# Attention passes: the last value products and the second copy-out moved into the next pass's first step

## What is computed

```python
q = q * cos + rotate_half(q) * sin
k = k * cos + rotate_half(k) * sin
scale = 1.0 / jnp.sqrt(jnp.asarray(HD, x.dtype))
attn = jnp.einsum('bhqd,bhkd->bhqk', q, k) * scale
attn = jax.nn.softmax(attn, axis=-1)
out = jnp.einsum('bhqk,bhkd->bhqd', attn, v)
```

## Time and profile before

| | |
|---|---|
| median of three runs | 950.13 us (949.09 to 950.76) |
| the profiled execution | 949.47 us |
| its span, first to last instruction | 947.7 us |
| PE busy | 794.8 us, 84% of the span |
| DVE busy | 788.2 us, 83% |
| ACT busy | 680.6 us, 72% |
| POOL busy | 238.7 us, 25% |
| mean granted TensorE clock | 0.933 of full speed |
| attention passes in the span | from 70 us (first exponential) to 430 us (last copy-out) |

### The profile page before, as it was taken

One profiled execution on the slowest core, in us unless ns is written; L12 is line 12 of the kernel. 1 busy time (PEld: TensorE's weight loads), 2 busy tenths in 40 slices (PEclk: granted clock), 3 DMA queues, 4 the chain that ended last, 5 costly groups with the idle time before them and its releaser, 6 DMA issues.

```text
span 947.7 us, 12535 instructions
## 1 busy us (share of the span) xinstructions
PE 794.8 (84%) x4272; PEld 419.4 (44%) x4272; DVE 788.2 (83%) x746; ACT 680.6 (72%) x1300; POOL 238.7 (25%) x133
## 2 busy tenths in 40 slices
PE   5689999999999999985575774766667876999998
PEld 3312222212222222223543553655666765888886
DVE  5998898878888988885868989999989764787864
ACT  2407777767777777784455796999996756888884
POOL 3800000000000000010100357897977411222200
PEclk9859999989999999998688788999998998999999
DMA  4313223230123110002101144455544202211111
GB/s 130 100 31 98 77 75 101 67 103 17 43 71 101 35 37 12 13 12 61 45 0 32 63 163 151 159 200 177 180 170 143 91 0 98 82 67 67 44 45 45
DMA packets 41688, 75.97 MB, mean 80 GB/s; under 512 B 7584, under 2 KB 25352, under 8 KB 40856
## 3 DMA queue, kind: packets, MB, share of 16 engines
q1 hardware_dynamic: 41624, 75.17, 24.8%
HBM read 64.99 MB, written 8.85 MB: 78 GB/s over the span
## 4 chain that ended last, share of the span: by engine, by line
PE 58%; DVE 17%; ACT 16%; issue 6%; DMA 2%; POOL 1%; ACTq 0%; DVEq 0%; POOLq 0%; SPq 0%
PE ps L1570 14%; PE ps L1591 13%; ACT dtb L1008 8%; PE ps L1541 7%; PE ps L1843 6%; PE ps L1844 6%; PE ps L1845 6%; ACT abar L982 4%; DVE nmax L1175 2%; DVE hst L1310 2%; ACT prob L884 1%; PE ps L1644 1%; PE ps L1743 1%; PE ps L1530 1%; PE ps L1718 1%
## 5 line engine op out<-in xcount | busy, mean ns | idle before, releaser
L884 ACT ACTIVATE prob<-ps 128x512 f32<-128x512 f32 x512 | 264.4, 607 | 98.8 <-PE ps L1570 96.3
L1178 DVE TENSOR_REDUCE nmax_k<-ps 128x2 f32<-128x1024 f32 x224 | 262.4, 1220 | 37.9 <-PE ps L1541 36.7
L1570 PE MATMUL ps<-qs,ks 96*128 96x512 bf16 x512 | 163.2, 391 | 5.6 <-ACT prob L884 4.1
L811 POOL TENSOR_TENSOR hc<-hst,cbr 128x1024 f32<-128x1024 f32 x63 | 153.0, 2452 | 42.4 <-DVE hst L1310 23.8
L1310 DVE TENSOR_TENSOR_SCAN hst<-abar,ps 128x1024 f32<-128x1024 f32 x64 | 143.1, 2274 | 6.6 <-PE ps L1743 4.2
L1591 PE MATMUL ps<-prob,vq 128*16 128x512 f32 x1024 | 134.2, 601 | 0.8 <-ACT prob L884 0.7
L1420 DVE TENSOR_TENSOR act_l<-act_t,act_h 128x1024 fp32r<-128x1024 f32 x64 | 86.4, 1362 | 39.1 <-ACT act_h L1106 39.1
L1570 PEld LDWEIGHTS ps<-qs,ks 96*128 96x128 bf16 x512 | 40.2, 97 | 164.6 <-ACT prob L884 109.7
L1008 ACT ACTIVATE dtb<-dtxt,bt 128x128 f32<-128x128 f32 x352 | 107.5, 398 | 0.9 <-PE ps L1743 0.9
L1743 PE MATMUL ps<-ident,dtb 128*128 128x128 f32 x352 | 56.3, 303 | 57.2 <-DVE hst L1310 43.0
L1102 ACT ACTIVATE act_t<-ps,b1t 128x512 f32<-128x512 f32 x128 | 81.8, 681 | 31.3 <-PE ps L1845 31.3
(11 more groups left out here) (204 smaller groups left out, 1118.5 us busy)
## 6 DMA issues: line engine op xcount, KB each, us to landing
cbr<-s_dram SPq DMA_DIRECT2D x64, 512.0 KB, 4.0
gate<-c_dram SPq DMA_DIRECT2D x6, 1024.0 KB, 4.7
qs<-q_dram SPq DMA_DIRECT2D x16, 288.0 KB
ks<-k_dram SPq DMA_DIRECT2D x48, 96.0 KB
o_dram<-o_sb SPq DMA_DIRECT2D x16, 256.0 KB, 2.1
wf<-in_L_ffn_w SPq DMA_DIRECT2D x8, 256.0 KB, 5.1
wfq<-in_L_ffn_w SPq DMA_DIRECT2D x8, 256.0 KB, 5.3
gate<-c_dram SPq DMA_DIRECT2D x4, 512.0 KB, 4.3
```

Source lines behind the costliest of these rows:

```text
L811: nc.gpsimd.tensor_tensor(hc[:, m % RING], hst[:, m % RING], cbr[:, m % RING], ALU.mult).then_inc(s_hc, 1)
L884: nc.scalar.activation(prob[:, n % 8], ps[:, 4 + (first + n) % 3], ACT.Exp, scale=ATT_SCALE).then_inc(s_exp, 1)
L1178: nc.vector.tensor_reduce(nmax_k[:, half, kk, 2 * pair:2 * pair + 2, qt], ps[:, 2 * pair:2 * pair + 2, :], AX.X, ALU.max, negate=True).the ...
L1570: nc.tensor.matmul(ps[:, 4 + (first + n) % 3], ks[p][:, kt // 4, j, kt % 4 * P:(kt % 4 + 1) * P], qs[p][:, half, j, :], start=True, stop=T ...
```

## The change

Three things are moved. On PE the products of step 15 are issued in step 0 of the next pass, after its fourth score product and second look-ahead tile, as those of every other step; the last pass alone keeps them at its end. The score products 0 to 2 of a later pass get the wait for the exponential three before. On ACT the copy of the second half is made after the four exponentials of the next pass's step 0, and steps 0 and 1 of a later pass wait for products as all others do. And ACT's loop is laid otherwise: pass 0 stands in front of it, its two rounds hold the passes 1 to 3 and 4 to 6, and pass 7 stands behind it. The number of passes in the loop's body (three) and of rounds (two) is as before. The bank of a score tile is the same as before for each.

```diff
-            def one_pass(it, first, between={}):
+            def one_pass(it, first, earlier, between={}):
...
-                        if j == 0 and s >= 2:
+                        if j == 0 and (s >= 2 or earlier):

                             act.wait_ge(s_pv, STEPS * it + s - 1)
...
+                    if s == 0 and earlier:
+                        evacuate(it - 1, 1)
                     if s == KT:
                         evacuate(it, 0)
-                evacuate(it, 1)
...
+            one_pass(0, 0, False)
             with act.Fori(0, PASSES // SETS) as r:
                 for p in range(SETS):
-                    one_pass(SETS * r + p, 4 * STEPS * p)
-            one_pass(PASSES - 2, 0)
+                    one_pass(SETS * r + p + 1, 4 * STEPS * (p + 1), True)
...
-            one_pass(PASSES - 1, 4 * STEPS, {
+            one_pass(PASSES - 1, 4 * STEPS * (PASSES - 1), True, {
                 8: lambda: norm_act(1, 0),
                 13: turned_weights})
+            evacuate(PASSES - 1, 1)
...
-                        if n >= 3:
+                        if n >= 3 or it:
                             pe.wait_ge(s_exp, 4 * STEPS * it + n - 2)
...
-                        if s >= 1 and j == (QUAD - 1 if todo else QUAD - 2):
-                            products(it, p, s - 1)
-                products(it, p, STEPS - 1)
+                        if j == (QUAD - 1 if todo else QUAD - 2):
+                            if s:
+                                products(it, p, s - 1)
+                            elif it:
+                                products(it - 1, (p - 1) % SETS, STEPS - 1)
+                if not more:
+                    products(it, p, STEPS - 1)
```

## The result

The changed kernel takes 945.71 us in the median of 8 runs (945.22 to 948.06), the kernel before 950.87 us in 8 (949.09 to 955.58). The ratio is 0.9951, with a 95% interval of 0.9935 to 0.9966: by the ratio 4.7 us faster, by the two medians 5.2, where 3.6 were forecast. In the profiled executions the span went from 947.7 to 944.1 us, by 3.6.

What follows compares the result with a forecast made beforehand. PE was taken to set the attention's pace, losing most at ACT's loop jump. Against the median, 950.13 - 3.59 (3.31 jump, 0.28 ordinary boundaries) = 946.5 us; range 944.9 to 949.2 us, own case 945.5 to 947.7.

Steps and rivals of the forecast that it cites:

- What bounds the kernel, and where the gain lies: PE sets attention's pace; the boundary from pass 2 to 3, at ACT's loop jump, costs 4.79 us more.
- The price of the jump in its new place: ACT's loop jump, now between passes 3 and 4, costs 1.48 us instead of 4.79: 3.31 us gained.
- The clock in the new gap: PE's gap of about 1.4 us at the moved jump leaves the clock at 1.00, no fall.
- Rival A: The clock falls in the new gap too: 2.54 us come back, gain 1.05, 949.1 us; chance 0.12.
- Ordinary boundaries: Seven pass boundaries go from 0.32 to 0.28 us each: 0.28 us gained; bounds 0 and 2.2.
- Passes in the loop and outside: Pass 6 gains up to 0.96 us inside ACT's loop, pass 0 loses as much outside: zero, within 0.3.
- The sum: Whole kernel: 949.47 - 3.31 - 0.28 = 945.9 us against the profiled execution, 946.5 against the median.
- All that comes behind shifts along: Everything behind the attention follows from its end and moves with it; no size of its own.
- D, late rows of maxima: A pass's first score, 0.98 us earlier, waits for its maxima: at full size 953.4 us, slower; chance 0.04.
- B, a second fetch: Jump dearer in its new place by a second or slower fetch: at most 2.1 us more, 948.6 us; chance 0.06.
- C, a hidden fetch: Fetch at the moved jump costs nothing: 4.79 + 0.28 us gained, 945.1 us; chance 0.08.
- E: Nothing moves: the jump's stall stays whole wherever it is and takes the clock down, 949.9 us; chance 0.03.

Runs made afterwards that it cites:

- b_one_round: Kernel before with ACT's loop over passes 0 to 5 made one round of six passes, no jump back; ratio to before 1.0008.
- b_relaid: Kernel before with only the changed kernel's loop layout (pass 0 in front, rounds of passes 1 to 3 and 4 to 6); ratio to before 0.9996.
- after_again: The changed kernel as it is, measured once more; ratio to before 0.9953.
- a_gap4_more: Changed kernel without ACT's loop and second wait, plus four copies and a shorter one before pass 4's first exponential; one run, attention 328.7 us.
- the pair without loop: Changed kernel and kernel before, each with ACT's passes written out and one wait per exponential; ratios to before 0.9918 and 0.9970.
- a_copy_only: Changed kernel with PE's old order, step 15's products at the pass's end, so only ACT's half of the change; ratio to before 1.0006.
- a_one_round: Changed kernel with ACT's loop made one round of six passes, no jump back; ratio to before 0.9987.
- a_one_wait: Changed kernel with ACT's passes 0 to 6 written out and no wait for products before a step's first exponential; 942.87 us, ratio to before 0.9918.
- a_gap5: a_one_wait with five added copies on ACT before pass 4's first exponential; one run, attention 334.7 us.
- a_gap5_again: Same program as a_gap5, run once more; one run, attention 329.0 us.
- b_products_only: Kernel before with only PE's half, step 15's products behind the third score of the next pass's step 0; one run, attention 350.0 us.

## Why the prediction was right, point by point

**What bounds the kernel, and where the gain lies.** Right. The distance between the copies of passes 2 and 3 went from 48.63 to 43.79 us, the 4.79 that the prediction had found and the 0.05 of an ordinary boundary, and b_one_round and b_relaid show that the jump is its cause: without a jump no such boundary, and with the jump elsewhere the price is elsewhere. One thing stays unshown: 2.5 of the 4.79 us were the fallen clock, and that is seen in one profiled execution of the kernel before. The fall does not come behind every such gap, so how much of it is in each of the other runs is not known.

**The price of the jump in its new place**: forecast 1.48, measured 1.0 (44.79 against 43.79), and 1.16 in after_again. ACT is idle for 1.70 us, where 2.1 were forecast, and PE for 0.89, where 1.4 were. The step that was off counted the fetch from the start of the instruction in front of the jump to the exponential behind, 2.72 us. Now it is shorter: the last of the four exponentials before starts at about 244.16 + 1.47 = 245.63, the next at 247.93, 2.30 us later (2.47 in after_again). The first instruction packet comes 1.7 us ahead of the exponential behind the jump at both places (204.3 before 206.05, and 246.2 before 247.93), but 1.0 us behind the start of the copy and 0.6 behind that of the last exponential: so if these packets are ACT's, the fetch begins earlier against ACT's work and is not shorter. An explanation is that the exponential in front waits in ACT's queue, so that the sequencer is at the jump before it starts, while the copy stood right before it; that was not tried by itself. This term alone is 0.48 us of gain above the forecast.

**The clock in the new gap.** No fall, as forecast, but the reason given was weak, and luck had a part. It argued from the scan's gaps of 1.48 and 1.80 us that one of 1.4 would do no harm. The gap came out at 0.89 (1.06 in after_again), shorter than any behind which a fall was seen; at the forecast's length one execution (a_gap4_more, 1.35) kept the clock, which by that run's expectation would make the step right, but behind 1.21 it fell three times in six. Rival A was worth more than 0.12 at the size forecast. Before the change the fall was part of the price both times that it was looked at (2.5 us in the earlier trace rows, 1.5 in b_relaid).

**Ordinary boundaries**: forecast 0.04 us each, measured 43.84 - 43.79 = 0.05 inside the loop, and 0.12 in the pair without loop. Small, as forecast; the 0.12 is three times the forecast, and still within its bounds of 0 to 0.32.

**Passes in the loop and outside**: forecast to cancel, within 0.3. They do: pass 0 lost 0.5 us up to pass 1's first copy (the copies are 0.18 later and then 0.42, with the first exponential 0.09 earlier), the passes 5 to 7 gained 0.6 (364.43 and 410.22 became 360.35 and 405.93, 4.08 and 4.29 earlier, against 3.70 at pass 5's). The steps of pass 0 show it, in ACT's timeline of the changed kernel:

```profile
93.44 2.06 ACT L884 ACTIVATE prob<-ps 128x512 f32<-128x512 f32 x4 [0.70 <-PE ps L1572]
```

That the reason is a second wait, the prediction did not know; it took the difference from rows without a cause, and so missed that removing it everywhere is worth more attention time (5.7 us) than the change itself (4.3 to 4.5).

**The sum.** The attention ends at 425.48 instead of 429.77 us: 4.3 us gained against 3.6 forecast, the difference being the jump's term (0.48) and the few hundredths of each boundary. "All that comes behind shifts along" holds only roughly: the span shows 3.6, as 0.7 us were lost behind it. The gate and up products' last copy is still 4.36 earlier, the last expert activation starts 3.6 earlier (935.8 and 932.2); between them the clock takes another course (its line on the page differs from slice 20 on), as it does between two executions of the same kernel. Why the medians differ by 5.2 us, more than the attention does, is not settled, nor why a_copy_only shows nothing of its 2.3 us. The range is also narrower than its own bounds: from 945.5 to 947.7 us was given for "the bounds of the jump and of the loop's passes", but a jump at its upper bound, 4.79 us instead of 1.48, would give 946.5 + 3.3 = 949.8.

**The rivals.** D, late rows of maxima: no wait of PE before the first score of a pass; the products of step 14 run straight into it, 245.46 and 246.44 above. B, a second fetch: a second instruction packet does come, in 248 to 249 us, but it costs nothing, as the exponentials behind the jump follow each other without a gap; b_relaid, with the loop at the same place, has its second one too, in 250 to 251. C, a hidden fetch: not hidden, though a_copy_only comes near with 0.41 us, not because ACT waits less (1.90 us of idle) but because PE has step 15's products to do meanwhile. E fell with b_relaid and the changed kernel side by side.

## What to carry to other kernels

When a stall's length is fixed, look at what stands between the last work in front of it and the first behind it: here the same jump cost 4.8 us (2.5 of them a fallen clock) behind a copy that came last on its engine, and 1.0 to 1.2 behind the exponentials. Count the waits of the instruction that starts the critical step of an inner loop: leaving out one that the order of another engine implies already was worth more (5.7 us of attention between a_one_round and a_one_wait, which have no loop) than the whole reordering; against the changed kernel, whose loop hides most of it, it was worth 2.5. And moving one engine's half alone can be worse than nothing: PE's half cost 15.9 us in its one run, while ACT's gained 2.3.

## What the runs showed of the hardware

- Outside the loop, where a step's first exponential has a second wait in front of it, it starts 0.06 us later than with one: idle 0.70 against 0.64 us a step, 44.48 against 43.64 us a pass (a_one_round and a_one_wait). Inside the loop of the changed kernel it is 0.64 with both waits.
- The jump back of ACT's loop of three passes leaves ACT idle for 2.12 and 2.29 us behind a copy (before, b_relaid), and for 1.70, 1.86 and 1.90 us, 1.06 to 1.26 more than usual, behind exponentials (changed, after_again, a_copy_only). The Trainium skill, "Runtime: NRT & Kernel Launch", Instruction fetch mechanics, says that a taken branch to a target outside the two pages held has to fetch it before execution goes on. The traces agree: an instruction packet comes in each of the gaps that were looked at (204.3, 246.2, 247.3 and 248.2 us in before, changed, a_copy_only and b_relaid), and b_one_round and a_one_round, without the jump, have neither the gap nor a packet there.
- The clock fell from 2.4 to 1.2 GHz behind idle times of PE of 1.21 to 3.32 us, and did not behind others of up to 1.66. With the same program and place it did both (1.67 and 1.66 us in a_gap5 and a_gap5_again), and with the same 1.21 us at six boundaries of one execution (b_products_only) it fell at three. How long it stayed down also varied: from about 3 us (b_relaid) to over ten (a_gap5).
